# A gated recurrent layer's order of work: every chunk two steps sooner, roots ahead of sigmoids, statistics ahead of the scan

## The reference, cut to what matters

```python
x = x + _L3_attn_ref(_layernorm(x), ...)
# in _L3_attn_ref:
residual = x
xn = rms_norm(x, g1)
lin = xn @ W_lin.T + b_lin
x_gel = gelu(lin)
x_rg = lin @ W_conv.T + b_conv
# rg_lru(x_rg):
rt = sigmoid(x_rg @ Wa.T + ba)
it = sigmoid(x_rg @ Wx.T + bx)
a = exp(-softplus(-Lam) * rt / 8)
gated = sqrt(1 - a * a) * (it * x_rg)
h[t] = a[t] * h[t-1] + gated[t]              # over the 256 tokens of a batch element
xr = (x_gel * h) @ W_lin2.T + b_lin2
residual = xr + residual
xm = rms_norm(residual, g2)
combined = gelu(sigmoid(xm @ W1.T + b1)) * (xm @ W2.T + b2)
return combined @ W3.T + b3 + residual
```

## Time and profile before

| | us |
|---|---|
| timed runs, median of 3 | 4033.36 (4030.43 to 4033.4) |
| profiled execution, own time | 4026.82 |
| its span in the profile | 4025.0 |

### The profile page before, as it was taken

One profiled execution on the slowest core, in us unless ns is written; L12 is line 12 of the kernel. 1 busy time (PEld: TensorE's weight loads), 2 busy tenths in 40 slices (PEclk: granted clock), 3 DMA queues, 4 the chain that ended last, 5 costly groups with the idle time before them and its releaser, 6 DMA issues. The chain is left out here.

```text
span 4025.0 us, 57539 instructions
## 1 busy us (share of the span) xinstructions
PE 3659.1 (91%) x19954; PEld 2561.8 (64%) x19954; DVE 3051.2 (76%) x7083; ACT 2290.5 (57%) x5549; POOL 1369.6 (34%) x880
## 2 busy tenths in 40 slices
PE   6888888999899989999999998888898889879998
PEld 2334334344566778997888896555566558646787
DVE  7999989999787767667788776677577784565777
ACT  7577766776665522224555557578677652264446
POOL 4989888999100000001232223475221200030000
PEclk8999999999999999999999998799899999989999
DMA  5555555657421000000000001000000000100000
GB/s 147 160 153 162 166 157 176 190 183 239 168 88 40 27 35 22 22 11 15 1 1 1 1 1 44 15 1 1 13 2 1 20 24 1 46 0 22 1 1 22
DMA packets 144441, 239.84 MB, mean 60 GB/s; under 512 B 23335, under 2 KB 67119, under 8 KB 141463
## 3 DMA queue, kind: packets, MB, share of 16 engines
q1 hardware_dynamic: 113475, 212.22, 17.1%
q10 hardware_dynamic: 30676, 23.93, 1.8%
HBM read 209.56 MB, written 26.54 MB: 59 GB/s over the span
## 5 line engine op out<-in xcount | busy, mean ns | idle before, releaser
L1293 DVE TENSOR_TENSOR_SCAN db<-PS,db 128x512 f32<-128x512 f32 x512 | 591.6, 1205 | 47.6 <-ACT PS L1258 34.6
L209 PE MATMUL PS<-db,cst 128*128 128x512 f32 x1024 | 498.0, 626 | 26.2 <-DVE db L1298 26.2
L216 PE MATMUL PS<-cst,p 128*128 128x128 f32 (+1 forms) x2880 | 396.5, 283 | 47.9 <-DVE pt L3526 16.7
L2264 POOL TENSOR_TENSOR rb<-rb,tb 128x512 f32<-128x512 f32 x32 | 42.9, 1342 | 1095.0 <-DVE tb L2259 1095.0
L216 PEld LDWEIGHTS PS<-cst,p 128*128 128x128 f32 (+1 forms) x2880 | 331.1, 147 | 121.0 <-issue 56.2
L209 PEld LDWEIGHTS PS<-db,cst 128*128 128x128 f32 x1024 | 201.6, 201 | 287.4 <-issue 234.1
L209 PE MATMUL PS<-xnT,W 128*128 128x256 f32 (+2 forms) x880 | 326.9, 514 | 44.5 <-ACT gate L1090 15.3
L1239 POOL TENSOR_TENSOR db<-W,b 128x1024 f32<-128x1024 f32 x128 | 307.3, 2425 | 58.0 <-DVE W L1175 44.9
L1239 POOL TENSOR_TENSOR db<-du,b 128x1024 f32<-128x1024 f32 x128 | 305.7, 2412 | 38.0 <-PE PS L209 37.3
L209 PEld LDWEIGHTS PS<-xnT,W 128*128 128x128 f32 (+1 forms) x880 | 169.8, 198 | 173.1 <-issue 113.9
L2115 ACT ACTIVATE W<-PS,W 128x512 f32<-128x512 f32 x144 | 98.8, 689 | 289.7 <-PE PS L209 272.5
(11 more groups left out here) (475 smaller groups left out, 8446.8 us busy)
## 6 DMA issues: line engine op xcount, KB each, us to landing
b<-bc_rows SPq DMA_DIRECT2D x256, 256.0 KB, 3.8
c<-bc_rows SPq DMA_DIRECT2D x256, 256.0 KB, 4.0
qk<-fore_qk SPq DMA_DIRECT2D x48, 294.5 KB, 2.9
fore_qk<-W ACTq DMA_DIRECT2D x48, 256.0 KB, 4.2
W<-in_we SPq DMA_DIRECT2D x9, 1024.0 KB, 4.9
W<-in_w SPq DMA_DIRECT2D x50, 128.0 KB, 3.8
fore_v<-W ACTq DMA_DIRECT2D x24, 256.0 KB, 3.0
v<-fore_v SPq DMA_DIRECT2D x6, 1024.0 KB
```

The lines of the kernel that those rows point to most:

```text
L209: ins = T.matmul(out, l, r, start=first and i == 0, stop=last and i == len(pairs) - 1)
L216: ins = T.transpose(bank[0:m, c:c + r], s, ident[0:r, 0:r])
L1293: V.tensor_tensor_scan(db[:, f, r], self.ring.PS[:, self.BANKS[x % 3], r], db[:, f, r], 0.0, ALU.mult, ALU.add).then_inc(self.sc.sem, 1)
L2264: e.eng.tensor_tensor(self.rb[t % 2], self.rb[t % 2], self.tb[t % len(self.tb)], ALU.add).then_inc(self.rg.sem, 1)
```

## The change

It computes the same and has the same instructions, less three table loads on ACT. It moves them:

- `start` is [-6, -4, -2, 0]: each chunk is two steps sooner, and the layer has two steps fewer. `Signs` calls the steps from f = 1 on. Phases 0 to 5 of chunk 0, 0 to 3 of chunk 1 and 0 and 1 of chunk 2 now lie inside the layer ahead. The buffer `xr` that chunk 0 uses first lies in cnT, which outlives that layer; so do the statistics of chunks 2 and 3.
- ACT: in a step, gelu comes first, then the small roots of phases 4 and 14, then the root of phase 10, then sigmoids, exp and the root of phase 1. Before: exp, gelu with root, sigmoids, small roots.
- DVE: the second and third statistics (3, 13) come ahead of the evacuations (6, 7), of 1 - a*a (9) and of the scan (11); 9 comes ahead of 11.
- POOL: the row additions are phase 8, ahead of the gate product, and wait for PE's gate product a of their chunk.
- PE: linear, conv and gate product x (6, 7, 8) come ahead of the output product (12).

```diff
@@ in Signs.act and Signs.dve
-                if self.follow and i == 7 and f > 2:
+                if self.follow and i == 7 and f:
...
@@ class Gated
-    ACT_ORDER = (9, 10, 8, 1, 4, 14)
-    DVE_ORDER = (5, 15, 6, 7, 11, 9, 0, 2, 3, 13, 12, 17, 18)
+    GEL, SQ = 10, 10.5
+    ACT_ORDER = (GEL, 4, 14, SQ, 8, 9, 1)
+    DVE_ORDER = (5, 15, 3, 13, 6, 7, 9, 11, 0, 2, 12, 17, 18)
...
-        self.st = E.stat + [E.tile(f"st{i}_9", 64) for i in (2, 3)]
         cn = E.cnT.rearrange("p k n -> p (k n)")
-        self.xr = [a.rearrange("p (t d) -> p t d", t=4) for a in (cn[:, 0:1024], E.tile("xr", 1024))]
+        self.st = E.stat + [cn[:, 1024 + 64 * i:1088 + 64 * i] for i in range(2)]
+        self.xr = [a.rearrange("p (t d) -> p t d", t=4) for a in (E.tile("xr", 1024), cn[:, 0:1024])]
...
-        self.start = [-4, -2, 0, 2]
+        self.start = [-6, -4, -2, 0]
...
-        for x in (12, 6, 16, 7, 8, 17, 18):
+        for x in (6, 7, 8, 12, 16, 17, 18):
...
                     G.tensor_tensor(buf[4], buf[4], buf[2], ALU.mult).then_inc(self.qG.sem, 1)
+                elif p == 8:
                     e.wait_ge(*self.rowS(2))
+                    e.wait_ge(*self.pm["a"](2 * c + 1))
                     e.wait_ge(*self.xn(self.order(c, 3)))
...
-        elif p == 10:
+        elif p == self.GEL:
             e.wait_ge(*self.linD(2 * c + 2))
             if c == 3:
                 e.wait_ge(*self.yD(1))
             C.activation(buf[1], buf[0], ACT.Gelu).then_inc(self.gelA.sem, 1)
+        elif p == self.SQ:
             e.wait_ge(*self.oD(c + 1))
             C.activation(buf[5], buf[5], ACT.Sqrt).then_inc(self.sqA.sem, 1)
```

More of the change, by code:

```diff
@@ L4439, in setup @@
         else:
-            self.start = [s + 4 for s in self.start]
+            self.start = [s + 6 for s in self.start]
         self.steps = self.start[3] + self.PHASES + 4
@@ L4485, in act_step @@
             for c, p in now:
-                if p == x:
-                    self.act_phase(e, c, p)
+                if p == int(x):
+                    self.act_phase(e, c, x)
         for c, p in now:
@@ L4593, in pool @@
                 elif p == 12:
-                    e.wait_ge(*self.qG(2 * c + 2))
+                    e.wait_ge(*self.qG(2 * c + 1))
                     for j in range(4):
@@ L4776, in dve_phase @@
             e.wait_ge(*self.sqA(c + 1))
-            e.wait_ge(*self.qG(2 * c + 1))
+            e.wait_ge(*self.qG(2 * c + 2))
             V.tensor_tensor(buf[4], buf[4], buf[5], ALU.mult).then_inc(e.own, e.up())
```

## The result

| | before | changed |
|---|---|---|
| timed runs, median of 6 each | 4031.89 (4027.29 to 4034.75) | 4016.66 (4012.12 to 4023.06) |
| ratio, 95% interval | | 0.9965 [0.9952, 0.9978] |
| profiled execution, own time | 4026.82 | 4022.34 |
| its span | 4025.0 | 4020.5 |

The account below looks back on a forecast made before the run. TensorE, busy 91% of the span, bounds the kernel, so only its idle time pays; carrying the new order forward put the last output product 15.35 us sooner, 4033.4 - 15.3 = 4018 us, range 4010 to 4028.

Parts of the forecast that it names:

- The seam: Start of the gated layer: PE turns chunk 0 at 3493.75 against 3498.28, 4.5 us sooner, without the 5.42 us pause.
- Chunk 0's gate product: Steps 0 to 5: PE waits 2.4 us for DVE's conv evacuation; the product starts at 3508.5 against 3513.19.
- the bounds: What the trace doesn't show; for the layer's first 15 us, full speed to half clock, some 3 us.
- Chunks 2 and 3 without a wait: First turns with roots ahead of sigmoids: chunk 2 at 3522.2 against 3531.64, 9.4 us ahead; chunk 3 at 3537.05.
- Steps 6 to 8: Up to chunk 1's output product: 3.0 us of DVE-POOL alternation, a PE wait of 2.65, start 14.7 us ahead.
- the half-clock rival: Brief PE pauses keep 1.2 GHz at chunk 0's products and chunk 1's output product, losing 3 + 3: gain 9.3, 4024; chance 0.20.
- the sign I had named: Evidence that would show the forecast right: chunk 1's output product 13 to 17 us ahead.
- Steps 9 to 12: Chunk 0's second apply to the last output product: PE idle 8.3 and 6.8 us, last output product at 3600.85 against 3616.20.
- the clash: At chunk 0's second apply DVE waits for POOL's pieces: 7.8 us taken, from a free 1.5.
- The sum: Last output product 15.35 us sooner; taken off the median, 4033.4 - 15.3 = 4018.
- The one row that I held against the lower clock: A 2.50 us pause at 3485.02 in the old kernel, after which PE ran on at full clock.
- The slower rival: POOL becomes the bound: each of four scans waits 6.3 us for rows and gate product, 4043; chance 0.04 for slower.

Follow-up runs that it names:

- the shift alone: The kernel before with `start` two steps sooner and the buffers in cnT this needs, all orders within a step old: 4023.77 us, ratio 0.9984.
- few rows: The changed kernel with POOL's row additions cut to 8 features of one tile per chunk: 116.98 us from 64-matmul product to chunk 3's output product, against 118.46.
- the orders alone: The changed kernel with the old `start`, so only the new orders within a step: 4025.81 us, ratio 0.9985.

## Why the prediction was right, point by point

**The seam.** All times here count from the start of the 64-matmul product. Forecast: turn at once after the last sum, at 8.73, at full clock. Measured 8.42, after 0.58, in 1.09. Right, and the shift alone shows that it is the shift's. The 0.3 us by which the added work was to hold up PE's 64-matmul product did not come: it waits 2.50 in both kernels.

**Chunk 0's gate product.** Wait 2.4 forecast, 2.35 measured, released by DVE's evacuation as described. The clock, which I had put among the bounds at 3 us, did fall: 5.24 for 3.70, 1.5 us.

**Chunks 2 and 3 without a wait.** Right; with ACT's old order waits return, of 1.18 each. Their turns came at 38.53 and 53.84 instead of 37.2 and 52.0, the 1.5 of the clock and 0.44 before chunk 1's gate product.

**Steps 6 to 8.** Chunk 0's output product without a wait: right. I charged 3.0 for POOL's rows at chunk 2's square and had PE wait at chunk 1's y. The size was right and the place wrong: the small statistics lost 2.5 (0.89 + 1.92 less 2 x 0.16), the square 0.9 (2.12 for 1.22), together 3.4. Since the statistics now stand ahead of chunk 3's evacuation, the loss came out as the unforeseen 3.13 before chunk 3's gate products, and the forecast 2.65 before chunk 1's output product shrank to 0.36. It started at 82.93, forecast 80.9, and ran at full clock (3.72), so the half-clock rival came true in half its first place (1.5 of 3) and not in its second. Against the kernel before that is 12.7 ahead (95.65 less 82.93), just short of the sign I had named, 13 to 17.

**Steps 9 to 12.** From the last sum to the applied chunk 7.3 us (3584.99 to 3592.26), forecast 7.8; the clash is there in full, as the nearest row had it. Chunk 2's output product took 6.19 and not the 5.50 charged, the last wait was 1.36: 118.46 against 115.8.

**The sum.** Gain 12.7 by the traces for 15.35. Of the missing 2.6 the clock makes 2.2 (1.54 + 0.69); the mis-sized term is therefore the clock behind PE's waits: at chunk 0's gate product, which the sum had at full speed, with a bound of 3 us and no row for it, and at chunk 2's output product, which it had at 5.50. The one row that I held against the lower clock (2.50 at 3485.02) I had used for chunk 1's output product. It was weak: with few rows the same 2.50 was followed by 9.36 instead of 7.84. The timed medians, 15.2 apart, agree with 4018, but their interval, 9 to 19 us, would also have allowed the half-clock rival's 9.3; it is the traces that place the gain between the two. That the medians came out within 0.2 us of the forecast is luck. The slower rival is out: no gate product of POOL's ended later than DVE was ready for its scan.

**What I did not price.** I counted each place where statistics ahead delay something, but as parts of a sum that was positive. The question "and without this part?" was never put. With DVE's old order chunk 2 is turned without a wait although its second statistics stand behind the evacuation; PE had waited 2.35 us behind statistics whose early place gained nothing there.

## What to carry to other kernels

When a change moves several orders at once, carry each part through the replay alone as well: here a part that cost 10.75 us of the stretch was covered by others that gained, and undoing it was worth nearly as much again as the change. On DVE, what an idle PE waits for (an evacuation, a scan) goes ahead of statistics that only a later step reads. Put GpSimd's work whose inputs are long ready under DVE's batch-norm statistics or PSUM-reading work, which kept their times beside it here (1.41 at 3567.22, 1.40 at 3571.83), and keep it off DVE's two-input instructions and its TENSOR_SCALARs from SBUF. Short ones count too, since one of 0.16 us can wait out a GpSimd instruction of 2 us.

## What the runs showed of the hardware that I had not expected

- **The clock does not follow the length of one pause.** The wait of 3.13 us before chunk 3's gate products was followed by full clock in the changed kernel (7.13 for two products), and by half clock for part of them with the orders alone (8.83); with few rows a wait of 2.05 us was followed by 8.83 too. In the same run the wait of 2.50 before the 64-matmul product was followed by 9.36 us, and in all ten other executions by 7.83 or 7.84. After chunk 0's wait of 2.35 the product took 5.24 to 5.40 in five kernels whose seam was short, and 6.75 with the long seam. What decides between 7.13 and 8.83 at the same place these runs don't show; it is worth 1.7 us, and a forecast should carry it as a spread.
- **The same short pause, with and without a spell at the lower clock.** In layer 10 PE pauses for 1.44 us in both kernels. In the kernel before (3704.11) the clock then stood at 0.50 from 3706 to 3716 and a product of 16 matmuls took 6.51; in the changed kernel (3704.32) it stayed at 1.00 and the same product took 3.70. A stretch is to be compared with that in view before a difference of spans is laid to an edit.
- **DVE's small instructions wait for GpSimd like large ones:** two-input ones take 0.16 us alone and 0.89, 1.92 and 1.56 beside it; a TENSOR_SCALAR with one input 0.17 alone and 0.95 beside it.
